# The last two slots' expert outputs through TensorE: 0/1 matrices in place of a store and a gather, in both expert networks of a two-layer graph network

## The chip, the cores and the metric

One core of one Trainium2 chip runs the whole program. The metric is the device time of one execution in microseconds (us); lower is better. The kernel before takes 2298.26 us, the median of three runs (2295.8 to 2303.56).

## What is computed

A graph network with 625 nodes of 768 values each and two layers. Each layer adds a graph convolution and a mixer to the nodes, and then a mixture of experts. Only the experts are touched here. Layer 0's, cut to what matters (layer 1's has one hidden layer of 1152, and takes its gates from a softmax over all experts):

```python
scores = x @ Wg + bg                               # x: the nodes after a layer norm
topk_vals, topk_idx = jax.lax.top_k(scores, 2)     # each node chooses 2 of 8 experts
gates = jax.nn.softmax(topk_vals, axis=-1)
comb = einsum('bnk,bnke->bne', gates, one_hot(topk_idx, 8))
for e in range(8):
    h = gelu(x @ W1[e] + b1[e]); h = gelu(h @ W2[e] + b2[e])
    y = h @ W3[e] + b3[e]
    out = out + comb[..., e:e + 1] * y
```

## The kernel before

The nodes lie in `X` as five tiles of 128 rows (`TILES` = 5; the last has 113). The experts are computed by slots of 128 rows (`XSLOTS` = 17: one for each of 8 experts and 9 more that go where an expert has more rows). The layers of the program run one after the other, each engine with an instruction stream written by hand, in order, with semaphores between them. The experts of layer n go like this:

1. Routing. VectorE (DVE) picks the two experts of each node and works out the place of each choice: `place` (row in the slots), `gate` (its weight), `comb` (weights by expert), `slot_hot` (which expert a slot has, for the biases). TensorE (PE) inverts the map (L2622: which node is in row r of slot v), which DVE copies to `slot_node` (L1926); that raises `placed`. PE also transposes `comb` (L2626) and DVE copies it to `combT` (L1931, L1932, into the tile `scoresT`).
2. GpSimd (POOL) gathers the rows of each slot from DRAM, an indirect DMA each (L971), two slots ahead.
3. For each turn: PE transposes the slot's rows (L2654), ScalarE (ACT) copies the transposes rounded to fp32r (`xt_hi`, `hT_hi`, L1210), DVE takes the rest (`xt_lo`, `hT_lo`, L1956), and PE makes three matmuls for each product (L686, L689, L690: hi*hi, lo*hi, hi*lo). The weights come by SyncE's DMAs, ACT rounds them (L1201, `weight_hi`) and DVE takes the rest (L1946, `weight_lo`, 2.56 us for 2304 columns), in a ring of four. Turns overlap the layers of neighbouring slots: in a turn, layer 0's slot v+1 stands beside layer 1's slot v.
4. `output(v)`: DVE copies the slot's result from PSUM to `bias_rows` (L1964), and ACT's queue stores it to `slot_out` in DRAM (L1223).
5. After the last slot (16): PE multiplies `combT` with the experts' output biases (L2720, in f32, 20 records for 10 products), and DVE adds them to `X` (L1992, `x_rows`).
6. POOL waits for all 17 stores, then gathers two rows for each node (L979, ten indirect DMAs, two for each tile of nodes). DVE adds them to `X` scaled by `gate` (L2004, `expert_sums`), a tile at a time.

In layer 0 step 6 feeds the mixer at once: for each tile of nodes DVE adds the two gathered rows, takes the statistics (L1421), normalises (L2026, L2030), PE transposes, ACT and DVE split (`tile_lo`, L1465), and PE makes the products of Q. The mixer's first two weights (`U_MIX1`) are split by DVE (L1518) before the sums. In layer 1 step 6 is the end of the program: SyncE stores each tile of `X` to the output.

## Time and profile before

| what | value |
|---|---|
| median of three runs | 2298.26 us |
| profiled execution, its own time | 2301.38 us |
| its span in the trace | 2299.3 us |
| PE busy | 2094.5 us (91%) |
| DVE busy | 1431.8 us (62%) |
| ACT busy | 923.5 us (40%) |
| POOL busy | 445.6 us (19%) |
| layer 0's experts, first slot's transposes to last matmul | 1185.4 to 1336.9 us |
| layer 1's experts, first slot's transposes to last matmul | 1901.8 to 2271.3 us |

The profiled execution's time is the one that a sum of durations is made against. The share of busy time is an average over stages; what counts for this change is which wait ends last in four short stretches: the routing in both layers, and the end of the experts in both layers.

### The profile page before, as it was taken

The numbers are of one execution on the slowest core, as the hardware profiler recorded it, in microseconds if no ns is written. First come the engines' busy times: TensorE is split into PE (matmuls) and PEld (weight loads), VectorE is DVE, ScalarE is ACT, GpSimd is POOL, SyncE is SP. The second block draws the span as 40 slices with busy tenths as digits, with TensorE's granted clock in tenths as the row PEclk, the third lists the DMA queues.
The fourth block names the chain that finished last, engine by engine and source line by source line (L and its number), as shares of the span: only waits on it lengthen the run. The fifth ranks groups of instructions, "written<-read, shape, count | busy, mean of one in ns | idle before, by whom it ended". The sixth has DMA issues, their size and how long they took to land. (4 is left out here: it accounts for less than half of the span.)

```text
span 2299.3 us, 32297 instructions
## 1 busy us (share of the span) xinstructions
PE 2094.5 (91%) x12786; PEld 2017.8 (88%) x12786; DVE 1431.8 (62%) x2297; ACT 923.5 (40%) x1220; POOL 445.6 (19%) x238
## 2 busy tenths in 40 slices
PE   6999999999999999999959959878898968999996
PEld 5898999998999999999959949777788858999995
DVE  7655555555763233333369974267985688888885
ACT  2342255555441111111137722124613226777772
POOL 1574300000301434444012122210000002011102
PEclk9999999999999999999969979988999988999997
DMA  3212233333331211110059961110212038999995
GB/s 108 43 33 81 86 116 116 125 130 112 133 128 42 75 42 42 52 52 21 16 196 327 327 224 62 49 32 28 79 56 83 15 119 317 375 373 363 374 372 178
DMA packets 117264, 316.27 MB, mean 138 GB/s; under 512 B 14201, under 2 KB 82841, under 8 KB 101884
## 3 DMA queue, kind: packets, MB, share of 16 engines
q1 hardware_dynamic: 98346, 269.60, 32.8%
q0 software_dynamic: 6880, 21.37, 3.1%
q10 hardware_dynamic: 11890, 23.25, 2.9%
q8 instruction: 102, 1.67, 0.3%
q14 instruction: 46, 0.38, 0.0%
HBM read 278.22 MB, written 35.87 MB: 137 GB/s over the span
## 5 line engine op out<-in xcount | busy, mean ns | idle before, releaser
L686 PE MATMUL banks<-weight_hi,xt_hi 128*128 128x384 f32 (+2 forms) x2208 | 737.4, 334 | 38.6 <-DVE xt_lo L1465 15.2
L689 PE MATMUL banks<-weight_lo,xt_hi 128*128 128x384 f32 (+2 forms) x2208 | 722.3, 327 | 0.0
L690 PE MATMUL banks<-weight_hi,xt_lo 128*128 128x384 f32 (+2 forms) x2208 | 722.1, 327 | 0.0
L686 PEld LDWEIGHTS banks<-weight_hi,xt_hi 128*128 128x128 f32 x2208 | 422.4, 191 | 50.5 <-issue 19.9
L689 PEld LDWEIGHTS banks<-weight_lo,xt_hi 128*128 128x128 f32 x2208 | 422.3, 191 | 0.4 <-issue 0.2
L690 PEld LDWEIGHTS banks<-weight_hi,xt_lo 128*128 128x128 f32 x2208 | 421.8, 191 | 0.0
L1946 DVE TENSOR_TENSOR weight_lo<-weight_raw,weight_hi 128x2304 fp32r<-128x2304 f32 (+2 forms) x153 | 341.1, 2241 | 43.5 <-ACT weight_hi L1201 42.4
L1201 ACT ACTIVATE weight_hi<-weight_raw 128x2304 fp32r<-128x2304 f32 (+2 forms) x153 | 286.6, 1882 | 81.7 <-PE banks L686 53.7
L893 POOL TENSOR_TENSOR weight_hi<-weight_raw,columns 128x2304 fp32r<-128x2304 f32 x20 | 80.6, 4028 | 687.9 <-DMA weight_raw<-L_gnn_root_in 322.5
L1693 DVE TENSOR_TENSOR held_lo<-banks,held_hi 128x384 fp32r<-128x384 f32 x80 | 44.6, 558 | 213.0 <-ACT held_hi L1128 213.0
L2571 PE MATMUL banks<-held_hi,a_rel 128*128 128x384 f32 (+1 forms) x550 | 170.6, 338 | 3.5 <-ACT a_rel L1143 2.8
L2571 PE MATMUL banks<-held_lo,a_rel 128*128 128x384 f32 x550 | 168.0, 338 | 0.0
L1681 DVE TENSOR_TENSOR adj<-adj,banks 128x640 f32 x120 | 98.2, 819 | 96.9 <-PE banks L2548 96.3
L686 PE MATMUL banks<-weight_hi,hT_hi 128*128 128x384 f32 (+1 forms) x442 | 150.3, 340 | 7.4 <-DVE bias_rows L1964 4.7
L690 PE MATMUL banks<-weight_hi,hT_lo 128*128 128x384 f32 (+1 forms) x442 | 149.8, 339 | 0.0
L689 PE MATMUL banks<-weight_lo,hT_hi 128*128 128x384 f32 (+1 forms) x442 | 149.8, 339 | 0.0
L971 POOL DMA_INDIRECT slot_in<-node_rows,through x34 | 68.8, 2024 | 394.9 <-PE banks L2654 335.7
L1128 ACT ACTIVATE held_hi<-banks 128x384 fp32r<-128x384 f32 x80 | 39.4, 493 | 244.5 <-PE banks L690 244.5
L1143 ACT ACTIVATE a_rel<-adj 128x640 fp32r<-128x640 uint16 x80 | 58.4, 744 | 157.1 <-PE banks L2571 155.3
L895 POOL TENSOR_TENSOR weight_lo<-weight_raw,weight_hi 128x2304 fp32r<-128x2304 f32 x20 | 115.8, 5789 | 1.6
L926 POOL DMA_INDIRECT edges_sorted<-code_i,pos_i x80 | 98.0, 1225 | 93.1 <-DVE pos_i L1631 64.7
L2571 PEld LDWEIGHTS banks<-held_hi,a_rel 128*128 128x128 f32 x550 | 102.1, 188 | 4.1 <-DVE adj L1681 3.1
(418 smaller groups left out, 3584.3 us busy)
## 6 DMA issues: line engine op xcount, KB each, us to landing
weight_raw<-L_ffn_w_in SPq DMA_DIRECT2D x102, 1152.0 KB, 7.2
weight_raw<-L_gnn_W_in SPq DMA_DIRECT2D x32, 1152.0 KB
weight_raw<-L_ffn_W_in SPq DMA_DIRECT2D x17, 1152.0 KB
products<-bias_rows SPq DMA_DIRECT2D x80, 192.0 KB, 1.9
slot_out<-bias_rows ACTq DMA_DIRECT2D x34, 384.0 KB, 6.6
weight_raw<-L_ffn_W_in SPq DMA_DIRECT2D x17, 576.0 KB
product_back<-products SPq DMA_DIRECT2D x10, 960.0 KB, 4.7
weight_raw<-L_mix_w_qkv_in SPq DMA_DIRECT2D x6, 1152.0 KB
```

What stands on the lines that cost most here:

```text
L686: ins = pe.matmul(dst, s[0], m[0], start=start, stop=False)
L689: pe.matmul(dst, s[0], m[1], start=False, stop=False)
L690: return pe.matmul(dst, s[1], m[0], start=False, stop=stop)
L893: pool.tensor_tensor(hi, raw[s][0:rows, 0:n], zero_col[0:rows, :].broadcast_to([rows, n]), ALU.add).then_inc(hi_ready, 1)
L895: pool.tensor_tensor(lo, raw[s][0:rows, 0:n], f32(hi), ALU.subtract).then_inc(unit_ready, 1)
L926: pool.indirect_dma_start(out=sorted_dram, out_offset=bass.IndirectOffsetOnAxis(ap=pos_i[:, c:c + 1], axis=0), in_=code_i[:, c:c + 1], in_ ...
L971: pool.indirect_dma_start(out=slot_in[v % 2][:, :], out_offset=None, in_=node_rows_dram, in_offset=bass.IndirectOffsetOnAxis(ap=slot_node[ ...
L1143: act.activation(A_r[:, t, :, :], adj[:, r * TILES:(r + 1) * TILES, t * P:(t + 1) * P], ACT.Copy).then_inc(a_ready, 1)
L1201: act.activation(W4[buffer][0][0:rows, col:col + k * cols], RAW4[buffer][0:rows, col:col + k * cols], ACT.Copy).then_inc(e_hi[n], 1)
L1681: vec.tensor_tensor(block_of, block_of, ps[:, 2 * (s % 2):2 * (s % 2) + 2, 0:HALF], ALU.add).then_inc(slot_done, 1)
L1946: vec.tensor_tensor(lo, RAW4[buffer][0:rows, col:col + k * cols], f32(hi), ALU.subtract).then_inc(e_lo[n], 1)
L2571: ins = pe.matmul(ps[:, agg_bank(m), 0:cols], A_r[:, t, src, :], part[:, src, 0:cols], start=begin, stop=end)
```

## The change

The outputs of slots 15 and 16 (`LATE` = 2) are no longer stored and gathered. `STORED` = 15 slots are. For the two late ones ACT and DVE read the result from PSUM, scaled by the gate of each row (`gate_row`), as a hi and a lo part (`late_out`), and PE multiplies them with a 0/1 matrix (`late_row`: which node each row of the slot belongs to) onto the products of the output biases, which DVE adds to `X` (`late_sums`). A choice in a late slot has gate 0 in the gathered sums and place 0. The gathers wait for the stores of slots 0 to 14 alone, and land in other buffers. The core of the diff:

```diff
+LATE = 2
+STORED = XSLOTS - LATE
 # GpSimd
+                pool.wait_ge(y_out[n][1], 16 * len(range(1, STORED, 2)))
+                pool.memset(out_b_f, 0.0).then_inc(cleared, 1)
+                for i in range(LATE):
+                    v = STORED + i
+                    pool.wait_ge(t_full[n], slot_groups(n, v))
+                    pool.iota(slot_in[v % 2][:, 0:COLS], [[1, COLS]], base=1, ...).then_inc(masks, 1)
                 for b in range(2):
-                    pool.wait_ge(y_out[n][b], 16 * len(range(b, XSLOTS, 2)))
+                    pool.wait_ge(y_out[n][b], 16 * len(range(b, STORED, 2)))
                 for t in range(TILES):
+                    if t == 2 + n:
+                        pool.wait_ge(t_full[n], t_groups(n))
+                    if n == 0 and t == 3:
+                        pool.wait_ge(e_lo[n], RAWS + SPLITS[n])
 # ScalarE
+                def late_out(v):
+                    i = v - STORED
+                    for c, (bank, cols, width) in enumerate(full_cols(n, last)):
+                        act.wait_ge(y_full[n], 2 * v + c + 1)
+                        act.activation(late_rows[i][0][:, cols], ps[:, bank, 0:width], ACT.Copy, scale=gate_row[:, i:i + 1]).then_inc(late_hi, 1)
...
+                        if i == 0 and turn == STORED:
+                            act.wait_ge(cleared, 16 + n + 1)
+                            for row in (0, EXPERTS, LOW_ROW):
+                                act.dma_start(out_b_f[row:row + EXPERTS, :], out_bias).then_inc(gate_in, 16)
 # VectorE, routing
+                order.step(vec.tensor_copy(comb_s[:, :, 0:EXPERTS], comb[:, :, :]))
+                order.step(vec.tensor_copy(comb_s[:, :, LOW_ROW:STACK], comb[:, :, :]))
...
+                order.step(vec.tensor_scalar(stored_f, slot_f, float(STORED), None, ALU.is_lt))
+                for i in range(LATE):
+                    ins = vec.scalar_tensor_tensor(late_gate[:, :, i], slot_f, float(STORED + i), flat_gate, ALU.is_equal, ALU.mult)
...
+                order.step(vec.tensor_tensor(place[:, :], place_f[:, :], stored_f, ALU.mult))
...
-                vec.wait_ge(comb_full, n + 1)
+                vec.wait_ge(routes_full, 2 * (n + 1))
...
+                vec.tensor_copy(gate_row, ps[:, COMB_BANKS[n][1], P:P + LATE]).then_inc(combT_ready, 1)
 # VectorE, end
+                for i in range(LATE):
+                    v = STORED + i
+                    vec.tensor_tensor(late_row[v % 2], slot_in[v % 2][:, 0:COLS], late_node[:, i:i + 1].broadcast_to([P, COLS]), ALU.is_equal)...
+                if n == 1:
+                    for t in range(FULL - 1):
+                        expert_sums(1, t)
+                late_out(XSLOTS - 1)
 # TensorE, routing
+                pe.wait_ge(comb_ready, 2 * (n + 1))
+                for j in range(CHOICES):
+                    ins = pe.matmul(ps[:, COMB_BANKS[n][1], P:P + LATE], f32(is_row[:, j, :]), late_gate[:, j, :], start=j == 0, stop=j == CHOICES - 1)
+                ins.then_inc(routes_full, 1)
 # TensorE, end
+                def from_slot(i, j, done):
+                    t, c = divmod(j, 2)
+                    for k, rows in enumerate(late_rows[i]):
+                        ins = pe.matmul(late_bank(j), late_row[(STORED + i) % 2][:, t * P:(t + 1) * P], rows[:, wcols(c)], start=False, stop=done and k == 1)
+                    return ins
+                for j in range(6):
+                    start(j)
+                for j in range(SET):
+                    if j >= 6:
+                        start(j)
+                    pe.wait_ge(y_used[n], 2 * (XSLOTS - 1) + j % 2 + 1)
+                    from_slot(1, j, True).then_inc(prod_full, 1)
```

`start(j)` is the product of the biases, now in fp32r with 40 rows, and the two products of slot 15. In layer 0 the mixer's loop changes too: the late sums of tiles 2 to 4 and the splits of the two `U_MIX1` weights stand between its tiles, behind the sums of tiles 0 and 1.

What moves on VectorE in the routing of layer 1, from the weights' selection to the first weight split. Before (`scoresT` is where `combT` lies, `through` is where `slot_node` lies):

```order
L1917 TENSOR_TENSOR gate_of<-is_chosen,comb 128x5x8 x2
L1924 TENSOR_REDUCE gate<-gate_of 128x10
L1926 CAST through<-banks 128x17
L1928 TENSOR_TENSOR slot_hot<-slot_expert_f,iota_p 128x2176
L1931 COPY scoresT<-banks 8x512
L1932 COPY scoresT<-banks 8x128
```

And now (`in_tile` holds `stored_f` and the late gates, `rank_of` the late slots' node numbers and gates):

```order
L1969 CAST weight_lo<-comb 128x5x8
L1970 CAST weight_lo<-comb 128x5x8
L1971 TENSOR_SCALAR weight_lo<-is_chosen 128x5x16
L1973 TENSOR_TENSOR gate_of<-is_chosen,comb 128x5x8 x2
L1975 TENSOR_TENSOR weight_lo<-comb,weight_lo 128x5x8
L1977 TENSOR_REDUCE gate<-gate_of 128x10
L1978 TENSOR_SCALAR in_tile<-more_of 128x10
L1981 SCALAR_TENSOR_TENSOR in_tile<-more_of,gate 128x10 x2
L1986 TENSOR_TENSOR place<-place_f,in_tile 128x10
L1989 TENSOR_TENSOR gate<-gate,in_tile 128x10
L1992 COPY rank_of<-banks 128x2
L1994 CAST through<-banks 128x17
```

Ten small instructions stand ahead of the one that releases the gathers of the slots. On TensorE the same stretch was, before:

```order
L2622 MATMUL banks<-weight_lo 128x18 x10
L2626 MATMUL banks<-ident,comb 8x128 x5
```

and has ten f32 matmuls more now, whose result VectorE waits for ahead of its copies and its first weight splits:

```order
L2731 MATMUL banks<-ident,weight_lo 40x128 x5
L2734 MATMUL banks<-in_tile,weight_lo 128x2 x10
```

VectorE at the end of layer 1, before, behind the last weight split:

```order
L1964 COPY bias_rows<-banks 128x384 x2
L1992 TENSOR_TENSOR x_rows<-banks,x_rows 128x384 x10
L2004 SCALAR_TENSOR_TENSOR x_rows<-xt_hi,gate,x_rows 128x768
L2004 SCALAR_TENSOR_TENSOR x_rows<-xt_lo,gate,x_rows 128x768
```

and now, where six gathered sums stand ahead of the last slot's output and four behind it:

```order
L2072 TENSOR_TENSOR late_row<-slot_in,rank_of 128x640 x2
L2074 CAST in_bias<-bias_rows 40x768
L2077 TENSOR_TENSOR in_bias<-bias_rows,in_bias 8x768
L2099 SCALAR_TENSOR_TENSOR x_rows<-xt_hi,gate,x_rows 128x768
L2099 SCALAR_TENSOR_TENSOR x_rows<-xt_lo,gate,x_rows 128x768
L2035 SCALAR_TENSOR_TENSOR hT_lo<-banks,rank_of,hT_hi 128x384 x2
L2099 SCALAR_TENSOR_TENSOR x_rows<-xt_hi,gate,x_rows 128x768
L2099 SCALAR_TENSOR_TENSOR x_rows<-xt_lo,gate,x_rows 128x768
L2107 TENSOR_TENSOR x_rows<-banks,x_rows 128x384 x10
```

(the pair of sums stands three times in the first place and twice in the second). VectorE in layer 0, in the mixer's loop, now:

```order
L2130 SCALAR_TENSOR_TENSOR q_rows<-q_rows,norms,mixer_in 128x768
L2107 TENSOR_TENSOR x_rows<-banks,x_rows 128x384 x6
L1571 TENSOR_TENSOR weight_lo<-weight_raw,weight_hi 128x2304
L1474 BN_STATS stats<-x_rows 128x6 x2
L1518 TENSOR_TENSOR xt_lo<-banks,xt_hi 128x3x128 x2
```

These six additions and the weight split (L1571; a second one stands behind tile 2) stood ahead of the first gathered sum before.

## Rows read from the trace of the kernel before

**Rows 1.** Busy us (instructions) of PE, PEld, DVE, ACT, POOL; PEclk, DMA share, GB/s.

```profile
2000.00:2050.00 50.00, 50.00 (x302) 50.00 (x301) 43.22 (x31) 36.85 (x33) 4.25 (x2) 1.00 0.97 386
```

**Rows 2.** The chain that ended last, its end: start us, us, what.

```profile
2287.04 7.03 DMA xt_lo<-slot_out,place
2295.14 1.02 DVE x_rows L2004
```

**Rows 3.** VectorE in order of time at the end: start, us, what, [idle before].

```profile
2260.64 2.56 DVE L1946 TENSOR_TENSOR weight_lo<-weight_raw,weight_hi 128x2304 fp32r<-128x2304 f32 x1 [0.36 <-ACT weight_hi L1201]
2270.83 1.02 DVE L1964 COPY bias_rows<-banks 128x384 f32<-128x384 f32 x2 [7.63 <-PE banks L690]
2272.43 1.85 DVE L1992 TENSOR_TENSOR x_rows<-banks,x_rows 128x384 f32<-128x384 f32 x3 [0.58 <-PE banks L2720]
```

**Rows 4.** ScalarE in order of time: the store of slot 14, the last weight split.

```profile
2247.78 0.33 ACTq L1223 DMA_DIRECT2D slot_out<-bias_rows  x1
2258.48 2.14 ACT L1201 ACTIVATE weight_hi<-weight_raw 128x2304 fp32r<-128x2304 f32 x1
```

**Rows 5.** The tile slot_out between 2240 and 2250 us: that store's landing.

```profile
DMA to landing us min/median/max: 6.0/6.0/6.0
```

**Rows 6.** GpSimd in order of time: gathers in layer 1 and in layer 0.

```profile
2274.45 0.94 POOL L979 DMA_INDIRECT xt_hi<-slot_out,place  x1 [90.08 <-DMA slot_out<-bias_rows]
2275.70 0.94 POOL L979 DMA_INDIRECT xt_lo<-slot_out,place  x1 [0.30 <-issue]
1346.82 2.68 POOL L979 DMA_INDIRECT v_rows<-slot_out,place  x1 [0.30 <-issue]
```

**Rows 7.** VectorE in order of time, routing of layer 1.

```profile
1891.17 1.49 DVE L1888 TENSOR_TENSOR weight_lo<-more_of,bias_rows 128x1280 fp32r<-128x1280 f32 x1
1895.31 0.18 DVE L1926 CAST through<-banks 128x17 int32<-128x17 f32 x1 [0.69 <-PE banks L2622]
1898.34 0.27 DVE L1932 COPY scoresT<-banks 8x128 f32<-8x128 f32 x1
1898.53 5.00 DVE L1946 TENSOR_TENSOR weight_lo<-weight_raw,weight_hi 128x2304 fp32r<-128x2304 f32 x2
```

**Rows 8.** TensorE in order of time, routing of layer 1.

```profile
1884.83 1.01 PE L2618 MATMUL banks<-is_chosen,ones_r 128*128 128x64 f32 x4
1892.97 2.31 PE L2622 MATMUL banks<-weight_lo 128*128 128x18 f32 x10 [7.12 <-DVE weight_lo L1891]
1895.13 1.23 PE L2626 MATMUL banks<-ident,comb 128*8 128x128 f32 x5
1904.62 0.66 PE L686 MATMUL banks<-weight_hi,xt_hi 128*128 128x384 f32 x1 [0.36 <-DVE xt_lo L1956]
```

**Rows 9.** The columns of rows 1, two us after a pause of PE.

```profile
2260.00:2262.00 2.00, 2.00 (x7) 2.00 (x8) 1.64 (x2) 0.61 (x1) 0.00 (x0) 0.57 0.43 166
```

**Rows 10.** TensorE in order of time, layer 0: the second slot, the first Q product.

```profile
1193.82 1.57 PE L2654 MATMUL banks<-ident,slot_in 128*128 128x128 f32 x6 [1.51 <-DMA slot_in<-node_rows,through]
1363.22 0.66 PE L686 MATMUL banks<-weight_hi,xt_hi 128*128 128x384 f32 x1 [4.57 <-issue]
```

**Rows 11.** VectorE in order of time, end of layer 0's experts and mixer loop.

```profile
1329.92 2.56 DVE L1946 TENSOR_TENSOR weight_lo<-weight_raw,weight_hi 128x2304 fp32r<-128x2304 f32 x1 [2.50 <-ACT weight_hi L1201]
1336.50 1.02 DVE L1964 COPY bias_rows<-banks 128x384 f32<-128x384 f32 x2 [2.63 <-PE banks L690]
1351.44 1.02 DVE L2004 SCALAR_TENSOR_TENSOR x_rows<-v_rows,gate,x_rows 128x768 f32<-128x768 f32 x1 [0.30 <-issue]
1359.07 1.02 DVE L2004 SCALAR_TENSOR_TENSOR x_rows<-v_rows,gate,x_rows 128x768 f32<-128x768 f32 x1 [2.08 <-DMA wide_rows<-slot_out,place]
1370.31 1.02 DVE L1465 TENSOR_TENSOR xt_lo<-banks,xt_hi 128x384 fp32r<-128x384 f32 x2 [1.85 <-ACT xt_hi L1019]
1382.84 1.00 DVE L1465 TENSOR_TENSOR xt_lo<-banks,xt_hi 128x384 fp32r<-128x384 f32 x2
```

**Rows 12.** The columns of rows 1, one us of layer 0's end.

```profile
1330.00:1331.00 1.00, 0.81 (x6) 0.62 (x4) 1.00 (x1) 0.15 (x1) 0.00 (x0) 1.00 0.00 0
```

More of the change, by code:

```diff
@@ L324, in build @@
             W_more = [fe2(f"weight{s}", [P, UNIT]) for s in range(2, RING)]
+            with ExitStack() as first:
+                combT = allocator(first)[0]("combT", [STACK, COLS], F32R)
             scoresT = fe("scoresT", [EXPERTS, COLS], F32)
@@ L376, in build @@
                 XE = allocator(first)[0]("xe_rows", [P, TILES, DIM], F32)
+            with ExitStack() as first:
+                late_hi_rows = allocator(first)[0]("late_hi_rows", [P, HID1], F32R)
             h_rows = fe("h_rows", [P, HID1], F32)
+            with ExitStack() as first:
+                late_row = [allocator(first)[0](f"late_row{s}", [P, DIM], F32R)[:, 0:COLS] for s in range(2)]
             slot_in = [fe(f"slot_in{s}", [P, DIM], F32) for s in range(2)]
@@ L1956, in transposed_lo, with late_out @@
                         vec.tensor_tensor(lo, t_source(n, l, bank, ks), f32(hi), ALU.subtract).then_inc(t_lo[n], 1)
+                def late_out(v):
+                    i = v - STORED
+                    if i == 0:
+                        vec.wait_ge(y_out[n][0], 16 * len(range(0, STORED, 2)))
+                    for c, (bank, cols, width) in enumerate(full_cols(n, last)):
+                        vec.wait_ge(late_hi, 2 * (LATE * n + i) + c + 1)
+                        hi, lo = late_rows[i]
+                        vec.scalar_tensor_tensor(lo[:, cols], ps[:, bank, 0:width], gate_row[:, i:i + 1], f32(hi[:, cols]), ALU.mult, ALU.subtract).then_inc(y_used[n], 1)
                 def output(v):
@@ L2003, in expert_sums, with late_sums @@
                 for k in range(CHOSEN):
-                    ins = vec.scalar_tensor_tensor(X[rows, t, :], out_rows[n][k][rows, t, :], gate[rows, t, k:k + 1], X[rows, t, :], ALU.mult, ALU.add)
-                    if n == 0 or k == 0:
-                        order.step(ins)
-                        order.wait()
-                    else:
-                        ins.then_inc(rows_done, 1)
+                    order.step(vec.scalar_tensor_tensor(X[rows, t, :], gathered(n, k, t)[rows, :], gate[rows, t, k:k + 1], X[rows, t, :], ALU.mult, ALU.add))
+                    order.wait()
+            def late_sums(n, t):
+                for c in range(2):
+                    j = 2 * t + c
+                    vec.wait_ge(prod_full, PR_FFN[n] + j + 1)
+                    ins = vec.tensor_tensor(X[:, t, wcols(c)], ps[:, LATE_BANKS[n][j % 8], 0:WCOL], X[:, t, wcols(c)], ALU.add)
+                    ins.then_inc(rows_done if n == 1 and c == 1 else prod_used, 1)
             experts(0)
@@ L2030, in _ @@
                 vec.scalar_tensor_tensor(XM[:, t, :], XM[:, t, :], rstd2[:, t:t + 1], in_shift, ALU.mult, ALU.add).then_inc(rows_ready, 1)
+                if t == 0:
+                    for tile in range(2, TILES):
+                        late_sums(0, tile)
+                    vec.wait_ge(prod_used, PR_FFN[0] + SET)
+                    unit_lo(U_MIX1)
+                elif t == 2:
+                    unit_lo(U_MIX1 + 1)
             vec.sem_inc(ln_var, TILES)
@@ L2337, in _ @@
             experts(1)
-            for t in range(TILES):
-                expert_sums(1, t)
             end_phase(vec, "vec", 7)
```

144 lines of the change are left out of this document (98 added, 46 removed).

## Prediction

> **What bounds the kernel now.** I read the windows of the experts first: in 50 us of layer 1's, PE is busy for all 50 and has the full clock, 2.4 GHz, while DVE is busy for 43 and DMA for 97% [rows 1]. So inside the slots nothing is to be had but by less PE work, of which the change takes none; what counts is where PE or the end waits. The chain that ended last shows that for the end: a gather of 7.03 us, then the last sum, over at 2296.16, and 3.1 us later (the output's store) the span's end at 2299.3 [rows 2]. DVE's order of time shows what stands there: PE is done with slot 16 at 2271.3, its output is copied at 2270.8, and from then to 2296.2 no expert work is done, 25 us for store, gathers and sums [rows 3]. The same wait stands in layer 0 ahead of the mixer, where DVE's first sum begins at 1351.44 though the last slot's copy began at 1336.50 [rows 11]; but there the 12.5 us between hold DVE work (bias sums, two weight splits). Then I read the two routings, where PE's first matmul waits for DVE [rows 7, 8].
>
> **Term 1, the end of layer 1: 11.5 us less.** Slot 14's store is issued at 2247.78 and lands 6.0 later, at 2253.8 [rows 4, 5]. Its landing now frees the gathers, where it was slot 16's: first gather about 2254.1 instead of 2274.45. The issues follow each other every 1.25 us [rows 6], so ten would take 12.5 us. But beside DVE's split of a weight one took 2.68 us [rows 6], and here DVE splits until 2255.7 and again from 2260.6 [rows 3]; I take 18 us, last issue about 2271 to 2272, last landing with 5.4 us from its end (7.03 less the 1.68 of the issue; [rows 2]) at 2277 to 2278. The Trainium skill (SBUF — State Buffer, SBUF: two separate sides) speaks against the change here: a GpSimd DMA's descriptors cannot be written while DVE holds the port pair that both use, for the whole of its instruction. The trace shows a slowdown, 2.68 against 0.94 us, and 18 us is my reading of it; by the rule in full the ten would take the 27 us of rival A, and the sum would be that rival's.
>
> DVE's order then makes the end. Its last weight split starts 1 us late, since ACT now rounds slot 15's output ahead of L1201 at 2258.48 [rows 4]: over at 2264.1. Two comparisons of 640 columns cost 1.5 us (1.49 us for 1280, [rows 7]), the bias rows 1.6 (bounds 1 and 2.2, by a 768-column operation of 1.0 each): 2267.2. Six gathered sums, 1.0 us each at their pitch [rows 2], end at 2273.2; PE is done at 2271.3, so slot 16's output waits 2 us for DVE and is over at 2274.2. Four sums make 2278.2, ten late sums 4.8 more (three in 1.85 less the tail, that is 0.48 each at their pitch, [rows 3]): 2283.0. PE's 50 products, of 0.18 us each at full clock, lie beside this: 18 run by 2274.6, and no sum of DVE waits for the rest, also at half clock. With 3.1 us for the store: 2286.1. Five stores within 4 us instead of 11, and tile 4's gather landing late, add up to 1.7: 2287.8 against 2299.3. Bounds: 9 less (the gathers take 21 us) and 13.5 less.
>
> **Term 2, the routing of layer 1: 4 us more.** Two things are added. Ten small DVE instructions stand ahead of the copy that releases the slots' gathers (L1926 at 1895.31); at 0.1 to 0.2 us each they make 1.6 us, of which 0.7 was a wait for PE anyway [rows 7]: 0.9 us. The greater one is PE's: ten f32 matmuls with 128x128 weights, whose result DVE must have before it copies `combT` and splits the first weights. An f32 matmul leaves two records: the four in [rows 8] at L2618 are two matmuls and last 1.01, a pitch of 0.22 as that of L2622 too (2.31 for ten). So twenty records are 4.4 us, behind the transposes that end at 1896.3: 1900.7. DVE, ready at 1898.7, waits, copies for 0.9 and begins the splits at 1901.6 instead of 1898.53 [rows 7]; PE's first matmul, at 1904.62, waits for what DVE does behind them: 3.1 us more. Then the clock. After 2 us of pause PE ran at 0.57, mostly at 1.2 GHz [rows 9]; here 3.4 us of pause come in ahead of 1904.62, where it ran at full clock after one matmul [rows 8]. That costs 0 to 2.6 us (18 matmuls by 0.144); I take 0.9. Nothing later gives the 3.1 us back, as PE has no pause inside the slots [rows 1]. Bounds: 1 (the ten matmuls cost little, so only the 0.9 is left) and 6.
>
> **Term 3, the routing of layer 0: 1 us more.** The same additions, but the second slot's transposes wait 1.51 us for their gather there [rows 10], and that gather is issued beside an idle DVE now, so it does not come later by as much. Of 2.4 us at the first matmul 1 is left. Bounds 0.5 and 2.5.
>
> **Term 4, the end of layer 0: 1.6 us less.** Slot 14's store lands by 1330, when the DMA share is 0 [rows 12]. Gathers run from about 1329.9, ten of them, not finished until 1345 (slowed by the split at 1329.92, [rows 11], and by the mixer's weights in the DMA queues). Tile 0's lands at 1340, tile 1's at 1343.6 (7.1 us behind its issue's end, as 1351.96 to 1359.07 in [rows 6, 11]: the issue behind the one shown took 2.16). DVE is ready for them at 1338.1. Sums of tiles 0 and 1 to 1345.6, four late sums 1347.5, tile 0's statistics and norm 3.4: 1351. Then come what was hidden before and is not now: six late sums (2.9), a weight split (2.5), statistics and `tile_lo` 2.0: 1358.5. PE's first Q product starts there instead of 1363.22 [rows 10]. At the old half clock it takes 5.8 us, and DVE waits for ACT about as now (1.85, [rows 11]); the second split (2.5) and the sums of tiles 2 to 4 follow, and `tile_lo` of tile 3, at 1382.84 before, ends the stretch at 1381.2. 4.7 us of lead at its start become 1.6 at its end, since 5 us of splits and 3 of sums came out of the old gap, and two waits of 2.08 and 1.85 pay for some. Bounds: 4 less, 2 more (each us that tile 1 lands late is one).
>
> **The sum:** -11.5 + 4 + 1 - 1.6 = -8.1. The profiled execution took 2301.38, so 2293.3 for one like it; the median of the runs is 3.1 lower, 2298.26, so 2290.2. That is 0.35% faster; 0.3% is 6.9 us, about what a measurement of this kernel can tell from no change.
>
> **The rivals.**
> A. *The gathers starve beside DVE's splits,* an issue standing still while DVE reads two tiles of SBUF: 2.56 us for each of two splits and some 5 us for comparisons and sums, on top of 18 or so. For it: 2.68 against 0.94 us [rows 6]. Tile 2's then land after 2273, and as they stand ahead of slot 16's output in DVE's order, that and all behind it wait. At 27 us for ten, term 1 falls to 6.5, and tile 1 lands 2 us later in layer 0: -1.6 becomes 0.4. Sum -1.1 to -3: 2296. Against it: DVE has idle stretches there, 7.63 us behind the last split [rows 3]. 0.12.
> B. *The routing costs its upper bounds*, the clock included: +6 and +2.5 for 5: sum -4.6 at term 1's value: 2293.7. For it: [rows 9]. 0.14 beyond the likeliest case.
> C. *The routing is nearly free*: PE's matmuls of two columns run faster than the pitch of records with 18 and 64 columns, so DVE never waits. Terms 2 and 3 become 0.9 and 0.5: sum -11.7: 2286.6. Against it: those pitches are alike for 18 and 64 columns, so it isn't the columns that set them [rows 8]. 0.14.
> D. *Slower.* In layer 0 DVE's order now puts tile 1's sums ahead of the six late sums and both splits, so a late tile 1 is paid in full. It decides from where tile 1 lands 10 us later than I say, 1353.6: sum 0.3 or more, 2299. For it: four gathers behind a full DMA queue, with the mixer's weights ahead of them; tile 1 landed at 1359 before, though issued from 1346.82 [rows 6, 11]. With starved gathers at the end 2302. 0.05.
>
> **How the numbers follow.** The likeliest case, all terms near their values, has 0.55 and a range of its own of 2287.5 to 2293.5; two thirds of it (0.37) lie below 2291.4, the 0.3% line. With C, 0.14, that makes 0.51 for faster. Within 0.3%: the rest of the likeliest case, 0.18, A's 0.12 and B's 0.14, 0.44 in all. Slower is D, 0.05. The range leaves out D, the lower part of C and the upper part of A: 2285.5 to 2296.
>
> **What would show it.** Right: POOL's first L1021 gather about 2254 + 5 (the routings' shift) instead of 2274 + 5; DVE's six sums without a wait ahead of slot 16's output; DVE waiting some 2 us for PE in layer 1's routing ahead of the `combT` copies; PE's first expert matmul of layer 1 3 us later from the routing's start, some of them at half clock; the first Q product some 4.7 us earlier from the last expert matmul, `tile_lo` of tile 3 some 1.6 earlier. Wrong: gathers of 2 to 3 us throughout; a DVE wait for a gather ahead of slot 16's output; no wait in the routing. It would be most wrong if a store's landing, which I take at 6.0 and 2 us, came later with the gathers beside it, or if something inside the slots moved, which I cost at nothing because PE has no pause there.

## The result and the profile after

The changed kernel takes 2296.58 us in the median of 22 runs (2290.91 to 2302.6), against 2300.9 us (2295.8 to 2304.72) of the kernel before on the same chip: ratio 0.9983, 95% interval 0.9976 to 0.9990. That is 4.3 us less in the medians, where 8.1 were forecast. The forecast time of 2290.2 us was too low by 6.4 us, and the median lies 0.6 us above the range's upper end. Of these 6.4 us, 2.6 are the level of the kernel before (2300.9 us in 22 runs, where the forecast started from the 2298.26 us of three); the other 3.8 are the change's. The interval is clear of 1, but the gain is below the 0.3% that the forecast took as the line. The profiled execution took 2290.91 us (span 2289.1), the fastest of its 22; so the whole spans say little here, and I compare stretches between fixed marks.

Four marks serve: the routing's compare of 1280 columns in each layer (DVE, row 1 of [rows 7]; 1174.71 and 1891.17 before, 1172.87 and 1888.56 after), PE's first bias product behind layer 0's last slot, `tile_lo` of tile 3 in the mixer, and the transposes of slot 16's hidden rows in layer 1.

**The end of layer 1.** GpSimd in order of time, after; it answers to [rows 6]:

```profile
2257.95 0.96 POOL L1021 DMA_INDIRECT xt_hi<-slot_out,place  x1 [19.07 <-DMA slot_out<-bias_rows]
...
2264.22 2.88 POOL L1021 DMA_INDIRECT xt_lo<-slot_out,place  x1 [0.30 <-issue]
...
2271.57 1.62 POOL L1021 DMA_INDIRECT xt_lo<-slot_out,place  x1 [0.30 <-issue]
```

VectorE in order of time, after; it answers to [rows 3]:

```profile
2263.72 2.56 DVE L2015 TENSOR_TENSOR weight_lo<-weight_raw,weight_hi 128x2304 fp32r<-128x2304 f32 x1 [1.18 <-ACT weight_hi L1243]
...
2269.22 1.02 DVE L2099 SCALAR_TENSOR_TENSOR x_rows<-xt_hi,gate,x_rows 128x768 f32<-128x768 f32 x1
...
2275.56 1.14 DVE L2035 SCALAR_TENSOR_TENSOR hT_lo<-banks,rank_of,hT_hi 128x384 fp32r<-128x384 f32 x2
...
2280.83 4.74 DVE L2107 TENSOR_TENSOR x_rows<-banks,x_rows 128x384 f32<-128x384 f32 x10
```

DVE does not stand still for a gather any more: none of its sums has an idle time in brackets. The ten gathers take 15.2 us. The longest issue is the one that fell into DVE's split; the short ones began while DVE stood still or read PSUM, or at the very start of a sum. From slot 16's transposes (2258.94) the span's end is 30.2 us away, where it was 42.5: 12.3 us less.

**The end of layer 0.** ScalarE and VectorE in order of time, after; it answers to [rows 11]:

```profile
1336.65 2.13 ACT L1070 ACTIVATE weight_hi<-weight_raw 128x2304 fp32r<-128x2304 f32 x1 [5.19 <-DMA weight_raw<-L_mix_w_qkv_in]
1345.98 2.12 ACT L1070 ACTIVATE weight_hi<-weight_raw 128x2304 fp32r<-128x2304 f32 x1 [7.20 <-DMA weight_raw<-L_mix_w_qkv_in]
1348.27 0.36 ACTq L1310 DMA_DIRECT2D out_gain<-L_mix_ln_out_g_in  x1
```

```profile
1334.79 1.02 DVE L2099 SCALAR_TENSOR_TENSOR x_rows<-xt_hi,gate,x_rows 128x768 f32<-128x768 f32 x1 [2.68 <-DMA xt_lo<-slot_out,place]
1337.70 1.02 DVE L2099 SCALAR_TENSOR_TENSOR x_rows<-xt_hi,gate,x_rows 128x768 f32<-128x768 f32 x1 [0.84 <-DMA xt_lo<-slot_out,place]
1339.81 1.95 DVE L2107 TENSOR_TENSOR x_rows<-banks,x_rows 128x384 f32<-128x384 f32 x4
1348.23 1.02 DVE L1474 BATCH_NORM_STATS2 stats<-x_rows 128x6 f32<-128x384 f32 x2 [6.47 <-ACTq L759]
```

The gathers come early, as meant: tile 0's sum begins at 1334.79, not 1351.44. But then DVE stands for 6.47 us with nothing left to sum. What it waits for is L759, the barrier between phases (`end_phase`), through which each engine passes only when the others have reached it. ACT reaches it late: its last act ahead of it is to round the mixer's second weight, which it waits 7.20 us for. That weight's DMA was issued at 1326.6 and is there at 1345.9, 19 us later; before, it was issued at 1332.8 and there by 1345.0, 12 us later, with none of the ten gathers beside it (the first was issued at 1344.3). The DMA view of 1326 to 1346 says what it shared the engines with:

```profile
q0 software_dynamic: 800, 3.93, 47.7%
q1 hardware_dynamic: 1568, 2.36, 34.3%
```

3.93 MB in q0 are the ten gathers, 2.36 MB in q1 the two weights. From the first bias product `tile_lo` of tile 3 stands 51.2 us off, where it was 45.7: 5.5 us more, where 1.6 less were forecast.

**The routings.** VectorE and TensorE in order of time, layer 1, after; it answers to [rows 7, 8]:

```profile
1893.27 0.18 DVE L1994 CAST through<-banks 128x17 int32<-128x17 f32 x1
1897.87 0.68 DVE L1999 CAST combT<-banks 40x512 fp32r<-40x512 f32 x1 [2.08 <-PE banks L2734]
1898.74 5.01 DVE L2015 TENSOR_TENSOR weight_lo<-weight_raw,weight_hi 128x2304 fp32r<-128x2304 f32 x2
```

```profile
1904.83 0.66 PE L717 MATMUL banks<-weight_hi,xt_hi 128*128 128x384 f32 x1 [2.32 <-DVE xt_lo L2025]
```

PE's first matmul stands 16.27 us behind the compare instead of 13.45. Its clock shows in windows of 3 us from 15 us behind the compare on, and in one window of the second slot (columns as in [rows 1]):

```profile
1903.56:1906.56 3.00, 1.73 (x5) 1.76 (x6) 3.00 (x4) 0.00 (x0) 1.01 (x1) 0.50 0.99 418
1906.56:1909.56 3.00, 3.00 (x11) 3.00 (x11) 0.58 (x1) 0.00 (x0) 0.00 (x0) 0.50 1.03 386
1909.56:1912.56 3.00, 3.00 (x18) 3.00 (x17) 0.00 (x0) 1.83 (x1) 0.00 (x0) 0.96 0.98 368
...
1920.06:1923.06 3.00, 3.00 (x13) 3.00 (x12) 3.00 (x3) 3.00 (x4) 0.00 (x0) 0.50 1.02 430
```

PE is busy for all of the second window but does 11 matmuls, where the third holds 18 (granted 0.96): granted 0.50, that is 1.2 GHz. Before, the granted clock was 1.00 in the window that begins 15 us behind the compare. The last window shows a second stretch at half clock, some 3 us long; the first profile of the kernel before has one too (0.50 from 1919.17 to 1922.17). By slot 16's transposes layer 1 is 4.7 us behind (370.4 against 365.6 us).

In layer 0, in contrast, the second slot's gather is issued in 0.96 us, not 3.84:

```profile
1181.97 0.96 POOL L1002 DMA_INDIRECT slot_in<-node_rows,through  x1 [0.31 <-issue]
```

PE no longer waits for its rows, its clock is full some 20 us behind the compare instead of 27, and the fifth slot's transposes come 38.6 us behind the compare, not 41.3.

So the traces of these two executions have two terms near their forecast (-12.3, +4.7), one of the other sign (+5.5) and one that should have been +1 and was a gain. The experiments ask which of these are the program's, and what each is made of.

### The profile page after: what moved, and what is told of

The parts are those of the page before. It is cut to its first block and busy times, and to the rows that moved or that the text cites. A ratio compares the mean times of both kernels' runs of the same rounds, so it can differ in the third digit from the quotient of the medians.

```text
span 2289.1 us, 32546 instructions
## 1 busy us (share of the span) xinstructions
PE 2105.3 (92%) x12886; PEld 2033.5 (89%) x12886; DVE 1433.6 (63%) x2327; ACT 926.2 (40%) x1228; POOL 441.1 (19%) x244
## 5 line engine op out<-in xcount | busy, mean ns | idle before, releaser
L2015 DVE TENSOR_TENSOR weight_lo<-weight_raw,weight_hi 128x2304 fp32r<-128x2304 f32 (+2 forms) x153 | 339.5, 2239 | 47.5 <-ACT weight_hi L1243 47.1
L1002 POOL DMA_INDIRECT slot_in<-node_rows,through x34 | 61.4, 1807 | 402.5 <-PE banks L2762 342.8
```

The lines of the kernel that those rows point to most:

```text
L1002: pool.indirect_dma_start(out=slot_in[v % 2][:, :], out_offset=None, in_=node_rows_dram, in_offset=bass.IndirectOffsetOnAxis(ap=slot_node[ ...
L2015: vec.tensor_tensor(lo, RAW4[buffer][0:rows, col:col + k * cols], f32(hi), ALU.subtract).then_inc(e_lo[n], 1)
```

## The experiments

Where no ratio is given, a kernel had one timed run and was made for its profile. Ratios are to the kernel before on the same chip.

**same_again, third_look: the changed kernel twice more.**

> The changed kernel once more, for a second profile and for its ratio beside the three kernels of this call. If the two stretches in which the first profile left the forecast are the program's own, this profile shows them again: routing of layer 0 to the last matmul of the experts 4 us shorter than before, and the end of layer 0 5.5 us longer, with a wait of DVE of 6 to 7 us ahead of the first BATCH_NORM_STATS2. If either was chance (the gathers' and weight loads' meeting on the DMA engines), it moves by over 2 us. Ratio to the kernel before 0.998.

> The changed kernel again, as the yardstick of this call: ratio to the kernel before 0.997 to 0.9985; the wait ahead of the first BATCH_NORM_STATS2 6 to 7 us; in layer 1 the fourth gather of the experts 41.5 us behind the compare of routing.

Ratios 0.9971 (0.9954 to 0.9987) and 0.9982 (0.9970 to 0.9995). Most marks repeat: the wait at the barrier is 6.35 us both times, `tile_lo` of tile 3 stands at 51.1 and 51.4 us, layer 0's fifth transposes at 38.6 and 38.7. In layer 1 the gather that follows the second slot's transposes stands at 41.5 us both times (41.6 in the first profile, 36.9 before). What did not repeat is layer 0's experts as a whole: from the compare to the first bias product 161.2 and 162.1 us, where the first profile had 158.2. The -4.3 that it seemed to show there was mostly the execution. same_again's start is later still: its compare stands at 1183.16, 10 us behind the first profile's, in a part that the change leaves alone.

**before_again: the kernel before once more.**

> The kernel before, profiled once more, beside kernels of the same chip. If the stretches around the change are the program's own, they come out as in the first profile: from the 1280-column compare of the routing to the second transposes 19.1 us and to the fifth 41.3 us in layer 0; to slot 16's transposes of the hidden rows 365.6 us and to DVE's last sum 405.0 us in layer 1. What differs between the two profiles of the whole then lies elsewhere, and the size of that difference is what no step of the change explains.

2308.76 us, where its neighbour on the chip took 2297.1 with the same program. Layer 0's marks repeat (18.6 and 40.9 us; bias products at 161.9 against 162.5; `tile_lo` of tile 3 at 45.4 against 45.7). So does the start of layer 1 (36.1 us; 36.9 in the first profile), and from slot 16's transposes to DVE's last sum both have 39.35 us. But slot 16's transposes come at 370.4, not 365.6: five of the later slots took 21.5 to 23.3 us in place of 21.15, with PE waiting for DVE, while the first profile has no such slots. The marks that failed the expectation are those of the whole layer: DVE's last sum stands at 409.7, not 405.0. So the kernel before can lose in layer 1 by itself as much as the change costs there.

**barrier_free: the second mixer weight is rounded behind the barrier.**

```
                     act.wait_ge(e_used[0], SPLITS[0])
-                    for c in range(2):
-                        unit_hi(U_MIX1 + c)
+                    unit_hi(U_MIX1)
...
                 tile_hi(TR_MIX_IN, t)
+                if t == 0:
+                    unit_hi(U_MIX1 + 1)
```

> ACT rounds the second mixer weight of layer 1 behind the phase barrier, after it has served tile 0's transposes, in place of just ahead of the barrier. Theory 1 (the early gathers delay this weight's load, and the barrier passes the delay on to all engines): DVE's wait of 6.5 us ahead of the first BATCH_NORM_STATS2 falls under 1 us, since PE's last product and DVE's late sums are done by 1342, and the kernel gains 5 to 6 us on the changed kernel: ratio 0.9955 to 0.9962 to the kernel before. Rival (the wait is replaced: tile 2's sum needs the gathers that the same DMA congestion delays, or DVE's remainder of that weight waits for ACT): the wait moves to a later line and the gain is 0 to 2 us, ratio 0.9975 to 0.9985.

VectorE in order of time, barrier_free:

```profile
1365.14 1.02 DVE L1475 BATCH_NORM_STATS2 stats<-x_rows 128x6 f32<-128x384 f32 x2 [3.72 <-PEq L759]
...
1399.52 1.02 DVE L1519 TENSOR_TENSOR xt_lo<-banks,xt_hi 128x384 fp32r<-128x384 f32 x2 [1.38 <-ACT xt_hi L1061]
```

The wait is not gone, it is 3.72 us and has another name, PEq, TensorE's sequencer: its 50 late products end last now. With the first bias product at 1352.36, `tile_lo` of tile 3 stands 47.2 us behind it, against 51.1 to 51.4: 4 us come back of 5.5. Neither expectation held in full. The weight's landing was the greater part, as the theory said, but the wait did not fall under 1 us; it was replaced, as the rival said, though by the late products, which neither had named. The ratio, 0.9982 (0.9965 to 0.9999), does not show it; this execution's compare of layer 0 stands at 1190.06, 17 us behind the first profile's.

**weights_first: tiles 2 to 4's gathers wait for that weight.**

```
+                    if n == 0 and t == 2:
+                        u = Unit(U_MIX1 + 1)
+                        pool.wait_ge(raw_ready[u.slot], u.loads)
```

> In layer 0 the six gathers of tiles 2 to 4 wait until the mixer's second weight has landed; the barrier is the changed kernel's. Theory (the ten gathers and the two weight loads share the DMA engines, which moves the weight's landing, ACT's rounding and so the barrier): the second weight lands 4 to 6 us earlier than its 19 us behind issue, DVE's wait ahead of the first BATCH_NORM_STATS2 falls from 6.5 to between 2.5 and 4 us, where TensorE's last late products end, the tiles 2 to 4 are there in time, and tile 3's remainder comes 3 to 4 us earlier: ratio 0.0015 below the changed kernel's. Rival (the weight is slow on its own account, or tile 2's rows now come too late for DVE's sums): the landing stays at 17 us or more, or a new wait stands ahead of tile 2's sums, and no time is won.

ScalarE, GpSimd and VectorE in order of time, weights_first:

```profile
1339.42 2.13 ACT L1073 ACTIVATE weight_hi<-weight_raw 128x2304 fp32r<-128x2304 f32 x1 [3.92 <-DMA weight_raw<-L_mix_w_qkv_in]
...
1342.95 2.13 ACT L1073 ACTIVATE weight_hi<-weight_raw 128x2304 fp32r<-128x2304 f32 x1 [1.40 <-DMA weight_raw<-L_mix_w_qkv_in]
```

```profile
1343.67 0.94 POOL L1024 DMA_INDIRECT v_rows<-slot_out,place  x1 [9.40 <-DMA weight_raw<-L_mix_w_qkv_in]
```

```profile
1347.96 1.02 DVE L1477 BATCH_NORM_STATS2 stats<-x_rows 128x6 f32<-128x384 f32 x2 [3.45 <-PEq L759]
...
1361.88 2.07 DVE L2102 SCALAR_TENSOR_TENSOR x_rows<-v_rows,gate,x_rows 128x768 f32<-128x768 f32 x2
```

Measured from the first bias product the second weight is rounded at 7.8 us instead of 14.9 (13.4 and 14.8 in the other two profiles); it lands 13.6 us behind its issue, not 19.4. Nothing in the barrier was changed, only what shares the DMA engines with the load; so the early gathers are what delayed it: 12 us with none of them beside the load, 13.6 with four, 19.4 with ten. Tile 2's sum at 1361.88 has no wait ahead of it: its rows, asked for 8 us later by the same mark, are in time. `tile_lo` of tile 3 stands at 47.1, as in barrier_free. Ratio 0.9970 (0.9958 to 0.9983), beside 0.9982 of third_look on the same chip.

**lows_first_1: in layer 1 DVE splits two weights ahead of the late gates' wait.**

```
+                for _ in range(FIRST_LO[n]):
+                    low()
                 vec.wait_ge(routes_full, 2 * (n + 1))
                 (three copies of combT and the gates)
-                for _ in range(FIRST_LO[n]):
-                    low()
                 transposed_lo(0, 0)
```

> In layer 1 alone DVE computes its first two weight remainders before it waits for the late gates' products and copies them, so that TensorE's 4.3 us of products for the late gates lie beside DVE's work. Theory (the cost of layer 1's routing is DVE's stall of 2.1 us behind those products, and the half clock that the longer pause brings): TensorE's first expert matmul comes 2 us earlier than in the changed kernel, the half clock at its start goes or shortens, and 2 to 4 us are gained: ratio 0.9965 to 0.9975. Rival (the transposes of the first slot's rows, which stand behind the same 20 products in TensorE's queue, or its gather, set the start): the first matmul moves by under 0.5 us and the time stays.

VectorE in order of time and the windows from 15 us behind the compare on and in the second slot, lows_first_1:

```profile
1913.26 5.02 DVE L2011 TENSOR_TENSOR weight_lo<-weight_raw,weight_hi 128x2304 fp32r<-128x2304 f32 x2
1918.19 0.67 DVE L2050 CAST combT<-banks 40x512 fp32r<-40x512 f32 x1
```

```profile
1921.11:1924.11 3.00, 3.00 (x11) 3.00 (x11) 1.55 (x1) 0.00 (x0) 0.00 (x0) 0.54 0.92 336
1924.11:1927.11 3.00, 3.00 (x19) 3.00 (x18) 0.00 (x0) 1.50 (x1) 0.00 (x0) 1.00 1.02 407
...
1937.61:1940.61 3.00, 3.00 (x20) 3.00 (x19) 3.00 (x5) 1.54 (x3) 0.00 (x0) 1.00 1.01 427
```

The copies have no wait now. PE's first matmul stands at 14.23 us, 2.0 earlier, and the clock is full 3 us sooner. The gather behind the second slot's transposes stands at 37.4 instead of 41.5, and slot 16's transposes at 366.1 instead of 370.3: 4.2 us come back, 2.0 by the stall and 2.2 more by the clock. The half clock behind the first matmul is shorter, and the second stretch of it, from 31 to 35 us, is not there. That stretch is worth 1.6 us: from the second slot's transposes to the third's it is 15.6 to 15.7 us in every profile that has it and 14.0 in every one that has not. It does not hang on the stall alone, since gathers_held_1, which is the changed kernel up to there, has not got it either (granted 1.00 from 1927.51 to 1930.51) and has slot 16's transposes at 368.6. At DVE's last sum the gain is 2.8: from slot 16's transposes to there this kernel takes 28.0 us, not 26.6, with TensorE granted 0.50 from 2275.45 to 2278.45, where the changed kernel has 1.00. (late_gates_short and all_three show 28.0 and such a stretch too, both_mended 26.6 and none.) Ratio 0.9969 (0.9952 to 0.9987), against 0.9971 of same_again on the same chip; its gain of 0.0018 does not show in it.

**late_gates_short: ten one-pass products for the late gates.**

```
+            late_gate = W_more[1][1][:, (behind comb_s)]
...
-  pe.matmul(ps[:, COMB_BANKS[n][1], P:P + LATE], f32(is_row[:, j, :]), late_gate[:, j, :], ...)
+  pe.matmul(ps[:, COMB_BANKS[n][1], P:P + LATE], is_row[:, j, :], late_gate[:, j, :], ...)
```

> The changed kernel, with the late gates' 10 products in the one-pass fp32r form, that is 10 instructions of TensorE in place of 20 (the gates of the late slots are rounded to what fp32r holds). Theory (DVE's stall is TensorE's time for these products): they take about 2.1 us in place of 4.3, DVE's wait of 1.9 to 2.1 us goes, and in layer 1 the first expert matmul comes 2 us earlier and slot 16's transposes 2 to 4 us earlier; in layer 0 the fifth transposes stay at 38.6 us if any work in the pause suffices for the clock, and go back towards 41 if it must be the full 4.3 us. Rival (waits of the products for their operands set their time): the wait shrinks by under 1 us.

TensorE and GpSimd in order of time, late_gates_short, layer 1 and layer 0:

```profile
1904.12 2.27 PE L2735 MATMUL banks<-weight_lo 128*128 128x2 f32 x10
```

```profile
1182.38 3.90 POOL L1003 DMA_INDIRECT slot_in<-node_rows,through  x1 [0.31 <-issue]
```

The products take 2.27 us, not 4.27. In layer 1 it is as theory says, and as with lows_first_1: first matmul at 14.14, slot 16's transposes at 366.1. Two different edits that take away the same 2 us of stall give the same 4.2 us, the absent stretch of half clock included. In layer 0 the gain turned into a loss: without DVE's wait its splits begin at 1181.96, ahead of the second gather and not behind it, and that gather is issued in 3.90 us again; the fifth transposes stand at 41.6 us instead of 38.7, and the bias products at 164.8 instead of 162. VectorE in order of time, late_gates_short, layer 0:

```profile
1181.96 3.48 DVE L2016 TENSOR_TENSOR weight_lo<-weight_raw,weight_hi 128x1152 fp32r<-128x1152 f32 x3
```

The splits end at 1185.44 and the gather's issue at 1186.28.

**lows_first_0: the same reordering as in lows_first_1, in layer 0 alone.**

> The same in layer 0 alone: three weight remainders ahead of the wait and the copies. Theory (in layer 0 the added stall of DVE was a gain in disguise: with DVE idle the second gather is issued in 1 us instead of 3.8, its rows come earlier, TensorE's pause between the first slots goes and its clock is full 8 us sooner, worth 4 to 5 us): the second gather is issued beside the remainders again, in 3 us or more, the wait ahead of the second transposes returns, and the kernel is 2 to 5 us slower than the changed one: ratio 0.9990 to 1.0005. Rival (the shorter stretch had nothing to do with it): the first matmul comes 1.5 to 2 us earlier, and the kernel gains as much: ratio 0.9975.

Neither side had it. The gather is issued in 0.96 us, though DVE's three splits (1190.00 to 1193.54) lie right beside it (1191.28 to 1192.24), and the fifth transposes stand at 39.0 us, 0.4 later than in the changed kernel. The first matmul comes 0.7 later, since three splits now stand ahead of it. Ratio 0.9984 (0.9968 to 1.0001). But the edit did not test what it was meant to: the gather was issued 0.07 us before the first split's end (1191.35), where those with 3.8 or 3.9 us were issued 0.4 to 0.5 us into it. So this kernel does not show that a busy DVE leaves the gather short.

**idle_filled: the kernel before, with 20 more products in PE's pause.**

```
                 ins.then_inc(comb_full, 1)
+                for j in range(CHOICES):
+                    pe.matmul(ps[:, 2, 0:2], ident[:, :], ident[:, 0:2], start=j == 0, stop=j == CHOICES - 1)
```

> The kernel before, with 20 more matrix products of TensorE (10 of float32 of two columns from the identity, into a bank that nothing reads) behind the transposes of the gates, where it waited 5.5 us for the first gather; nobody waits for them. Theory 1 (the changed kernel's products for the late gates brought TensorE's clock to full earlier in layer 0, 20 us behind the compare in place of 26): the clock rises early here too, and the fifth transposes stand at 38.6 to 39 us, as in the changed kernel. Rival (DVE's later remainders, which let the second gather be issued in 1.0 us in place of 3.8, did it): the fifth transposes stay at 41.3 us. In layer 1, where the changed kernel lost 4.7 us, theory 1 says no loss here.

The fifth transposes stay at 41.1 us, the second gather at 3.84, and the clock is 0.50 still in the window from 24 to 27 us. Work in that pause alone does nothing; theory 1 is out. In layer 1 the start is unchanged too (first matmul 13.45), though slot 16's transposes come at 373.2 us, with late slots like before_again's. From there to DVE's last sum this profile has 37.6 us, not 39.35; its granted clock is 1.00 from 2268.06 to 2271.06, where before_again has 0.50 from 2267.68 to 2270.68. Of all profiles, those with a short second gather in layer 0 have the fifth transposes at 38.6 to 39.1 us (the changed kernel and all of its variants but one) and those with a long one at 40.9 to 41.6 (the kernel before twice, idle_filled, late_gates_short). late_gates_short goes from one side to the other by an edit that shortens PE's products and so moves DVE's splits ahead of the gather; I did not force the gather's length by itself.

**gathers_held_1: layer 1's ten gathers wait for slot 16's products.**

```
+                if n == 1:
+                    pool.wait_ge(y_full[n], 2 * XSLOTS)
```

> In layer 1 alone the ten gathers wait until slot 16's products are done, as they did for its store before; everything else is the changed kernel. Theory (the gain at the end is the gathers' start beside slots 15 and 16): the gathers begin 11 us behind slot 16's transposes, end 15 us later, land 6 us after that, and DVE's last sum stands at 405 to 408 us behind the compare of routing in place of 397. Rival (the gain is mostly the store's two DMA latencies, and the gathers' place matters little because the late products take as long): the last sum stands at 397 to 401 us.

GpSimd and VectorE in order of time, and the waits of TensorE in this stretch (waiter, releaser, us, times, longest), gathers_held_1:

```profile
2278.30 0.97 POOL L1023 DMA_INDIRECT xt_hi<-slot_out,place  x1 [34.11 <-PE banks L721]
...
2290.12 0.95 POOL L1023 DMA_INDIRECT xt_lo<-slot_out,place  x1 [0.30 <-issue]
```

```profile
2297.69 4.27 DVE L2109 TENSOR_TENSOR x_rows<-banks,x_rows 128x384 f32<-128x384 f32 x9
```

```profile
PE banks L2836 <- DVE hT_lo L2037: 9.6, 1, 9.6
```

The last sum ends 38.5 us behind slot 16's transposes, against 26.6 in the changed kernel (three profiles) and 39.35 before (two profiles; 37.6 in idle_filled). The late products are there, the last store is not, and still at most 0.9 us of the gain is left: holding the gathers costs 11.9 us. Held gathers also held up PE's late products for 9.6 us, because DVE's sums stand ahead of slot 16's output in its order.

**both_mended, all_three: the edits that gave time back, together.** The first has barrier_free's and lows_first_1's, the second weights_first's too.

> Both single changes that shortened a stretch, together: the second mixer weight's rounding behind the barrier, and in layer 1 the two remainders ahead of the wait for the late gates. If they are independent, 3.9 us come back at the end of layer 0 and 4.2 us in layer 1, 8 us in all: ratio 0.9935 to 0.995 to the kernel before, 0.0035 below the changed kernel's. Rival (the other stretches' DMA waits take a share, as in the layer 0 experts, where an earlier start did not bring an earlier end): 3 to 5 us, ratio 0.996.

> The same, and the gathers of tiles 2 to 4 behind the weights as in weights_first. With the rounding behind the barrier the barrier waits for TensorE's late products alone (3.7 us), which neither edit moves, so theory says no more than 1 us beyond both_mended; less than that kernel's gain, if the later gathers bring a wait of tile 2's sums.

Ratios 0.9960 (0.9945 to 0.9976) and 0.9950 (0.9933 to 0.9967), on one chip with third_look's 0.9982 and weights_first's 0.9970. Medians: 2291.98 and 2289.17 us, against 2297.54 of the changed kernel and 2302.1 of the kernel before. both_mended is 5.6 us below the changed kernel in the medians, where 8 were expected: the two gains did not add up in full, as its rival had said (3 to 5 us, ratio 0.996). In all_three layer 1's slot 16 is at 366.0 us, and the barrier holds DVE for 3.58 us, for PE's late products:

```profile
1348.41 1.02 DVE L1478 BATCH_NORM_STATS2 stats<-x_rows 128x6 f32<-128x384 f32 x2 [3.58 <-PEq L759]
```

`tile_lo` of tile 3 is at 48.2 and 47.9 us, 1 us later than with either edit for the layer's end alone. all_three is the fastest kernel of this study, 0.5% below the kernel before; its median is 2.8 us below both_mended's, but the intervals overlap and do not show it to be faster.

## Why the forecast was wrong

**Term 1 (-11.5) was right.** The traces give -12.3 to the span's end, and to DVE's last sum -12.7, from two profiles of the kernel before and three of the changed one. Some of that is the clock's: both profiles of the kernel before ran at half clock for some 3 us behind slot 16's transposes, those of the changed kernel did not. Without that stretch on either side it is 37.6 (idle_filled) to 26.6, with it 39.35 to 28.0 (lows_first_1): 11 us less. gathers_held_1 shows that all of it hangs on the gathers' start. The ten took 15.2 us in the first profile (14.6 to 16.7 in all variants where they start early), not 18; rival A's 27 did not come. The Trainium skill (SBUF — State Buffer, SBUF: two separate sides) has GpSimd's descriptors wait for the whole of a DVE instruction that holds the shared ports. The trace agrees. The issue of 2.88 us ends at 2267.10, 0.82 us behind the end of the split (2266.28) that ran when it began; the 1.17 and 1.15 us behind it end 0.83 us behind a comparison (2267.74) and a bias row (2269.19), and the last, 1.62 us, 0.83 us behind a gathered sum (2272.36). In the fourteen profiles, from layer 0's routing on, 456 issues take more than 1.02 us, and each ends 0.81 to 0.89 us behind the end of a DVE instruction that reads two tiles of SBUF; the 119 that began in the midst of one that reads PSUM, with none of the first kind next to it, took 0.94 to 0.95 us. So the step "by the rule in full the ten would take the 27 us of rival A" was wrong: at this end an issue lost what was left of the instruction that it met, not all of DVE's work.

**Term 2 (+4) was right in its stall; its size rests on the profiles that it is taken from.** The late gates' products took 4.27 us for 20 records (4.4 forecast), DVE waited 2.08 us for them, PE's first matmul came 2.8 us later (3.1 forecast). The half clock there cost more than my 0.9: it lasted until some 4.9 us behind the first matmul, where before it was over after 0.7, which makes 2.1 us (an estimate: half of the 4.2 us more). Together that is 4.9, near the measured 4.7 at slot 16's transposes. At the gather behind the second slot's transposes it is 4.6 to 5.5 us against either profile of the kernel before. But at slot 16's transposes before_again stands where the changed kernel does, since its late slots were slower. The two experiments that took 2.0 us of stall away won 4.2, of which 1.6 is the second stretch of half clock.

**Term 3 (+1) had the wrong sign at the start, and hardly matters.** The prediction saw that "that gather is issued beside an idle DVE now, so it does not come later by as much", but did not price it: the issue is 2.9 us shorter (0.96 for 3.84 us). Before, it began 0.5 us into the first of three splits and ended 0.85 us behind the last; now it begins while DVE waits for the late gates. By the fifth slot layer 0 was 2.2 to 2.7 us ahead. But the experts did not keep it. Up to the bias products the kernel before has 162.5 and 161.9 us, the changed one 158.2, 161.2 and 162.1, its six variants with the same start 159.6 to 162.3. In these slots the DMA engines show a share of 0.96 to 1.02 (1250 to 1318 us, before and after), and from the sixth slot on PE waits 3.2 to 5.2 us in all for DVE, in varying places. I put what is left at about 1 us, an estimate from the means (161.1 of those nine, 162.2 of the two).

**Term 4 (-1.6) is the step that failed.** It was +5.5 in all three profiles. The prediction let DVE go from the four late sums straight to tile 0's statistics ("late sums 1347.5, tile 0's statistics and norm 3.4: 1351") and never passed the barrier that lies between. It saw the early gathers meet the mixer's weights in the DMA queues, but priced that for the gathers alone. Up to the four late sums it was right: they end 10.7 us behind the first bias product, where it had put them at 10.3. Then DVE stood for 6.47 us. The price fell on the other party: the second weight took 19 us instead of 12, ACT waits for it ahead of the barrier, and by the barrier so does everyone. Two edits that attack different links (the order of ACT's work, and who goes first on the DMA engines) each bring back 4 us, to the same limit, TensorE's late products, which this term had at nothing; in layer 0 they end some 3.6 us behind the last sum. The 1.5 us up to the old time I put down to them, which is argued and not shown. Rival D had the right place and the right sign, and named tile 1's gather as the culprit: that one landed by 1337.7, in good time.

**The sum** of the marks, against the first profile of the kernel before, is -12.3 + 4.7 - 1.1 + 5.5 = -3.2 us, beside 4.3 us between the medians and 3.9 by the ratio. With term 4 at its forecast it would have been -10.3. It comes out near the measured time, but some of its parts do not repeat to the microsecond: 1.4 to 1.8 of the -12.3 are the clock's, and the 4.7 is not there against before_again.

**Still open:** which gather gets in between two splits. Nine of the 456 long issues waited for the second or third DVE instruction in a row, among them the 3.84 us of layer 0's second gather; in lows_first_1 and two more kernels, one in layer 1 got in behind the first of two (2.13 us). Open too is why a stretch of half clock comes in the second slot of layer 1 in some executions and not in others.

## What to carry to other kernels

When a transfer is moved earlier, list every load that is in flight in its new place and follow each of those to its consumer, through barriers too: a barrier turns one engine's late load into everyone's wait. Put in front of a barrier only what the phase behind it needs at once. And a gain read off one pair of profiles should be checked between marks that a second profile repeats, and at the same granted clock: here most stretches held to 0.5 us from one execution to the next, but the start of layer 1 moved by 2 us with a stretch of half clock, and the whole by ten.

## What the runs showed of the hardware

- Ten gathers (3.93 MB) and two weight loads (2.36 MB) together kept the DMA engines 80 to 85% busy over 20 us, and the second load took 19 us; it took 13.6 us with four of the gathers beside it, and 12 us with none.
- The issue of a gather by GpSimd takes 0.94 to 0.96 us beside an idle DVE or one that reads PSUM. If it begins while a DVE instruction reads two tiles of SBUF, it ends 0.81 to 0.89 us behind the end of that instruction or, in nine of 456 cases, of a later one in the same row of instructions.
- A stall of 2.0 us more ahead of TensorE's first expert matmul of layer 1 cost 4.2 us by slot 16: the clock stayed at 1.2 GHz until 5 us behind that matmul, and, counted from the compare, was at 2.4 GHz 3 us sooner when the pause was shorter by 2 us. A further stretch at 1.2 GHz in the second slot, worth 1.6 us of the 4.2, came in six of the seven profiles with the stall and in none of the four without.
- Products with two columns and a 128x128 weight cost the same per record as those with 18 columns: 4.27 us for 20, 2.27 for 10, 2.30 for 10 with 18.
- Of one program, executions on one chip differed by 10 us and more (the kernel before: 2299.2 to 2319.48 us). The compare of layer 0's routing stands between 1172.87 and 1190.06 us in profiles of kernels that are the same up to there.
